# A 64-key by 96-query band for the product with V, a Newton step kept in PSUM, and a new table of places

## The reference

```python
def local_attention(q, k, v):          # window 32, 16 heads of 64
    # bk2, bv2: each window of 32 queries sees its own 32 keys and the 32 before
    mask = (it < jb) | (it > jb + w) | (jb == -1)
    sim = einsum('bhwie,bhwje->bhwij', bq, bk2) * 8.0
    sim = where(mask, -finfo.max, sim)
    attn = softmax(sim, -1)
    return einsum('bhwij,bhwje->bhwie', attn, bv2)

def ffn_layer(x, g, bln, W1, b1, W2, b2):
    mu = x.mean(-1); var = ((x - mu) ** 2).mean(-1)
    xn = (x - mu) / sqrt(var + 1e-05) * g + bln
    a, gate = split(xn @ W1 + b1, 2)
    return a * gelu(gate) @ W2 + b2

for i in range(6):
    x = attn_layer(shift_tokens(x), ...) + x
    x = ffn_layer(shift_tokens(x), ...) + x
```

## Time and profile before

| | |
|---|---|
| time, median of 3 | 3551.12 us (3550.79 to 3555.56) |
| span of the profiled execution | 3553.3 us |
| PE busy | 3325.9 us (94%), 65032 matmul records |
| DVE / ACT / POOL busy | 2737.3 (77%) / 2545.5 (72%) / 2041.5 us (57%) |
| granted clock of PE, mean | 0.984 of 2.4 GHz |
| stretch from 600 to 3500 us: PE, DVE, ACT, POOL | 2750.62, 2368.64, 2168.89, 1974.79 us of 2900 |

### The profile page before, as it was taken

One profiled execution on the slowest core, in us unless ns is written; L12 is line 12 of the kernel. 1 busy time (PEld: TensorE's weight loads), 2 busy tenths in 40 slices (PEclk: granted clock), 3 DMA queues, 4 the chain that ended last, 5 costly groups with the idle time before them and its releaser, 6 DMA issues.

```text
span 3553.3 us, 149054 instructions
## 1 busy us (share of the span) xinstructions
PE 3325.9 (94%) x65032; PEld 2107.6 (59%) x65032; DVE 2737.3 (77%) x3420; ACT 2545.5 (72%) x5866; POOL 2041.5 (57%) x1557
## 2 busy tenths in 40 slices
PE   7999987999999999999999999999999999999996
PEld 3444434666666666666666666666666666666663
DVE  3656557888887878888788878788888878788883
ACT  4667655777777777777777767677777777787774
POOL 0000006766676666766666666667676667676661
PEclk9999998999999999999999999999999999999998
DMA  3223224333333333433333333334333333333330
GB/s 109 76 71 84 75 61 141 135 127 127 134 133 133 118 127 130 140 131 129 119 122 136 130 124 127 127 124 143 126 130 126 121 136 125 135 127 131 129 122 24
DMA packets 247337, 423.34 MB, mean 119 GB/s; under 512 B 71966, under 2 KB 110108, under 8 KB 246556
## 3 DMA queue, kind: packets, MB, share of 16 engines
q1 hardware_dynamic: 220368, 397.28, 33.1%
q10 hardware_dynamic: 26316, 16.52, 1.6%
HBM read 124.21 MB, written 7.34 MB: 37 GB/s over the span
## 4 chain that ended last, share of the span: by engine, by line
PE 64%; DVE 17%; issue 7%; ACT 5%; POOL 5%; DMA 1%; SPq 1%; DVEq 0%; POOLq 0%; ACTq 0%
PE PS L535 64%; DVE TPB L932 5%; DVE MX L956 2%; ACT SC L1237 1%; DVE NV L947 1%; POOL K L1324 1%; POOL Q L1342 1%; DMA RB<-root_scratch 1%; POOL K L1342 1%; DVE PP L977 1%; DVE PX L978 1%; DVE NV L945 1%; DVE H L800 1%; DVE H L1000 1%; DVE NV L949 1%
## 5 line engine op out<-in xcount | busy, mean ns | idle before, releaser
L932 DVE SCALAR_TENSOR_TENSOR TPB<-PS,VEC,C 128x1024 f32<-128x1024 f32 x768 | 961.8, 1270 | 102.0 <-ACT SX L1213 95.0
L1237 ACT ACTIVATE SC<-PS,BQ,RQ 128x64 f32<-128x64 f32 x3072 | 979.5, 436 | 40.7 <-DVE BQ L961 40.3
L1213 ACT ACTIVATE SX<-PS 128x512 f32<-128x512 f32 x768 | 461.5, 620 | 391.4 <-PE PS L535 388.4
L1324 POOL TENSOR_TENSOR K<-K,RB 128x512 f32<-128x512 f32 x384 | 497.2, 1295 | 283.1 <-DMA RB<-root_scratch 278.4
L1347 POOL TENSOR_TENSOR SC<-SC,RC 128x1024 f32<-128x1024 f32 x192 | 366.3, 1908 | 480.2 <-DVE RC L969 478.8
L535 PEld LDWEIGHTS PS<-PP,VV 32*64 32x64 f32 x24576 | 433.7, 133 | 278.6 <-issue 276.3
L535 PE MATMUL PS<-PP,VV 32*64 32x64 f32 (+1 forms) x24576 | 541.2, 223 | 7.8 <-issue 6.2
L1342 POOL TENSOR_TENSOR K<-TPB,TR 128x512 f32<-128x512 f32 x384 | 496.4, 1293 | 0.0
L1342 POOL TENSOR_TENSOR Q<-TPB,TR 128x512 f32<-128x512 f32 x384 | 495.5, 1290 | 0.0
L535 PE MATMUL PS<-LXH,LH 128*128 128x512 f32 x768 | 371.3, 484 | 85.2 <-DVE TPB L932 68.4
L535 PE MATMUL PS<-K,Q 64*32 64x64 f32 (+1 forms) x24576 | 302.2, 224 | 49.5 <-issue 48.0
(11 more groups left out here) (167 smaller groups left out, 5809.8 us busy)
## 6 DMA issues: line engine op xcount, KB each, us to landing
TR<-TPB SPq DMA_DIRECT2D x768, 256.0 KB, 2.7
RB<-root_scratch SPq DMA_DIRECT2D x768, 128.0 KB
PP<-PX SPq DMA_DIRECT2D x192, 192.0 KB, 2.6
WS<-in_wqkv ACTq DMA_DIRECT2D x72, 128.0 KB, 2.4
PP<-PX SPq DMA_DIRECT2D x192, 48.0 KB, 2.5
QA<-TH SPq DMA_DIRECT2D x128, 64.0 KB, 2.1
QA<-TL SPq DMA_DIRECT2D x128, 64.0 KB, 2.1
KA<-TH SPq DMA_DIRECT2D x128, 64.0 KB, 2.1
```

Source lines behind the costliest of these rows:

```text
L932: e.scalar_tensor_tensor(TPB[:, n % 3:4 + n % 2:3 + n % 2 - n % 3, w, :], g, VEC[:, l, 9 + w:10 + w], C[:, at:at + 1024].rearrange("p (o c ...
L1213: e.activation(SX[i % 3][:, :], bk("PJ", key)[:, :], ACT.Square).then_inc(sem["pj_act"], 1)
L1237: p = e.activation(SC[m % 2][:, g, :, :].rearrange("p x k -> p (x k)"), bank[s][:, at:at + 64], ACT.Exp, bias=BQ[m % 2][:, g:g + 1], scale ...
L1324: e.tensor_tensor(dst, dst, RB[n % 2][:, :], ALU.mult).then_inc(sem["pr_pool"], 1)
```

## The change

Four things change.

1. **The band.** `PP` gets three places per head and window instead of two. Partitions 0 to 63 hold the 64 keys of windows j and j+1 (j even within its four), and the three places are the queries of windows j, j+1 and j+2: own keys and the keys before, with zeros in the two corners that a 64 by 96 block has and the band has not. POOL fills both PP with zeros once (before the first `NP`). Both transposes now write to tiles of their own, `PX[0]` and `PX[1]`, and SP carries both to PP: four DMAs of 32 partitions for the one and four for the other, instead of two DMAs.
2. **PV in two rounds** of 16 matmuls of 64 rows by 64 columns that move 96 columns (64 at the last window). The two row halves of a round write to different banks (`x = (t + rho) % 2`), and the second round swaps them. The matmuls of a step fall from 64 to 32, its records from 128 to 64.
3. **The feed-forward norm's Newton step in PSUM.** All three instructions of `rsqrt` write to the bank that F2 wrote; ACT's logarithm and exponential stay in H[0]; the tiles FX and EZ go. `F3` reads the root from the bank. So the bank is held until `F3` is through (`"f3_dve", u + 1`). The other layer norms use the same function: their first two results now stay in PSUM too, and their bank is held until the third instruction instead of the first.
4. **A new `PLACE` table**, with two places for PV instead of four.

```diff
-    "LS": 221.000, ... "PV": (4.410, 5.233, 5.448, 5.789), "PVn": 6.127,
+    "LS": 220.298, ... "PV": (4.733, 5.318), "PVn": 6.035,
...
-        o.put("N2", kind, b, banks=[(None, kind + "_root", 3, 1)])
-        o.keep(o.bank["N2", (kind, b), 0], kind + "_root", 3 * b + 1)
+        o.put("N2", kind, b, banks=[(None, kind + "_root", 3, 3)])
+        o.keep(o.bank["N2", (kind, b), 0], kind + "_root", 3 * b + 3)
...
-        lay(z + P["F2"], group, "F2", u, "f2_dve", 3 * u + 1)
+        lay(z + P["F2"], group, "F2", u, "f3_dve", u + 1)
...
-        PP = [sb(f"PP{i}", [128, 2, 16, 32]) for i in range(2)]
-        PX = sb("PX", [128, 16, 32])
+        PP = [sb(f"PP{i}", [128, 3, 16, 32]) for i in range(2)]
+        PX = [sb(f"PX{i}", [128, 16, 32]) for i in range(2)]
...
                 elif st == "PX":
                     m, = key
-                    a, z = PX, PP[m % 2]
+                    z = PP[m % 2]
+                    if m == 0:
+                        on.wait_ge("band_pool", 2)
                     if m > 1:
-                        on.wait_ge("pv_pe", 4 * m - 4)
+                        on.wait_ge("pv_pe", 2 * m - 2)
+                    on.wait_ge("tt_dve", 2 * m + 1)
+                    for r in range(4):
+                        k = slice(32 * r, 32 * r + 32)
+                        e.dma_start(z[k, r % 2, :, :], PX[0][k, :, :]).then_inc(sem[f"px_in{m % 2}"], 16)
                     on.wait_ge("tt_dve", 2 * m + 2)
-                    e.dma_start(z[0:96, 1, :, :], a[32:128, :, :]).then_inc(sem[f"px_in{m % 2}"], 16)
-                    e.dma_start(z[96:128, 1, :, :].rearrange("p (x c) a -> p x c a", c=4)[:, :, 0:3, :],
-                                a[0:32, :, :].rearrange("p (x c) a -> p x c a", c=4)[:, :, 1:4, :]).then_inc(sem[f"px_in{m % 2}"], 16)
+                    for r in range(1, 4):
+                        e.dma_start(z[32 * r - 32:32 * r, 1 + (r + 1) % 2, :, :],
+                                    PX[1][32 * r:32 * r + 32, :, :]).then_inc(sem[f"px_in{m % 2}"], 16)
+                    e.dma_start(z[96:128, 2, :, :].rearrange("p (x c) a -> p x c a", c=4)[:, :, 0:3, :],
+                                PX[1][0:32, :, :].rearrange("p (x c) a -> p x c a", c=4)[:, :, 1:4, :]).then_inc(sem[f"px_in{m % 2}"], 16)
...
                     for c in range(4):
-                        for x in range(2):
+                        for t in range(2):
                             for s in range(2):
-                                r = (rho + 2 * x + s) % 4
-                                j = 4 * c + r
-                                w = min(2, 16 - j)
+                                x = (t + rho) % 2
+                                j = 4 * c + 2 * t
+                                w = min(3, 16 - j)
                                 h = 2 * ((2 * p + x) % 8) + s
-                                y = mm(bank[2 + x][64 * s:64 * s + 64, 32 * j:32 * j + 32 * w],
-                                       VV[32 * r:32 * r + 32, c, 64 * h:64 * h + 64],
-                                       PP[p % 2][32 * r:32 * r + 32, 0:w, 8 * s + 4 * x + c, :],
-                                       rho == 0 and c == 0, rho == 3 and c == 3, skip_group_check=True)
+                                k = slice(64 * t, 64 * t + 64)
+                                y = mm(bank[2 + x][64 * s:64 * s + 64, 32 * j:32 * j + 32 * w], VV[k, c, 64 * h:64 * h + 64],
+                                       PP[p % 2][k, 0:w, 8 * s + 4 * x + c, :], rho == 0 and c == 0, rho == 1 and c == 3,
+                                       skip_group_check=True)
...
-            def rsqrt(v, u, x, step, done, r):
+            def rsqrt(v, x, y, step, done, r):
                 on.wait_ge(step, 2 * r + 2)
-                e.scalar_tensor_tensor(u, v, EPS, x, ALU.add, ALU.mult).then_inc(sem[done], 1)
+                e.scalar_tensor_tensor(v, v, EPS, x, ALU.add, ALU.mult).then_inc(sem[done], 1)
                 on.wait_ge(done, 3 * r + 1)
-                e.scalar_tensor_tensor(u, u, -0.5, x, ALU.mult, ALU.mult).then_inc(sem[done], 1)
+                e.scalar_tensor_tensor(v, v, -0.5, x, ALU.mult, ALU.mult).then_inc(sem[done], 1)
                 on.wait_ge(done, 3 * r + 2)
-                e.scalar_tensor_tensor(x, u, 1.5, x, ALU.add, ALU.mult).then_inc(sem[done], 1)
+                e.scalar_tensor_tensor(y, v, 1.5, x, ALU.add, ALU.mult).then_inc(sem[done], 1)
...
                     if m:
-                        on.wait_ge(f"px_in{(m - 1) % 2}", 32 * ((m - 1) // 2) + 32)
-                    if m > 1:
-                        on.wait_ge("pv_pe", 4 * m - 4)
+                        on.wait_ge(f"px_in{(m - 1) % 2}", 128 * ((m - 1) // 2) + 128)
                     on.wait_ge("np_pool", m + 1)
-                    e.transpose(PP[m % 2][:, 0, :, :], SC[m % 2][:, :, 1, :]).then_inc(sem["tt_dve"], 1)
-                    e.transpose(PX[:, :, :], SC[m % 2][:, :, 0, :]).then_inc(sem["tt_dve"], 1)
+                    e.transpose(PX[0][:, :, :], SC[m % 2][:, :, 1, :]).then_inc(sem["tt_dve"], 1)
+                    e.transpose(PX[1][:, :, :], SC[m % 2][:, :, 0, :]).then_inc(sem["tt_dve"], 1)
...
-                    rsqrt(bk("F2", key)[:, :], H[0][:, :], FX[:, :], "f2_act", "f2_dve", u)
+                    rsqrt(bk("F2", key)[:, :], H[0][:, :], bk("F2", key)[:, :], "f2_act", "f2_dve", u)
...
-                    e.tensor_tensor(H[2][:, :], H[1][:, :], FX[:, :], ALU.mult).then_inc(sem["f3_dve"], 1)
+                    e.tensor_tensor(H[2][:, :], H[1][:, :], bk("F2", key)[:, :], ALU.mult).then_inc(sem["f3_dve"], 1)
```

More of the change, by code:

```diff
@@ L29 @@
 PLACE = {
[13 rows of a table removed]
[8 rows of a table added]
+    "AQd": -0.283, "AV": (-11.276, -0.033), "AVa": -0.352, "AS": -1.210, "ASa": -1.501, "ASd": -1.358, "AY": 0.853,
+    "AE": 2.043, "AEa": 3.123, "AR": (14.319, 25.541), "AI": (24.544, 25.073, 27.040), "AM": (28.693, 0.806),
+    "AMd": -0.620, "AO": (30.433, 0.719), "NM": (36.253, 37.657, 37.185), "AZ": 39.606,
+    "NX": (43.040, 44.810, 45.102), "AW": 47.360,
 }
@@ L294, in order @@
                 lay(n + P["S3"][i], o.put, "S3", m, i)
+            for i in range(2):
                 lay(n + P["PV"][i], o.put, "PV", m, i)
@@ L379, in build @@
         ES = sb("ES", [128, L])
-        EZ = sb("EZ", [128, L])
         SC = [sb(f"SC{i}", [128, 16, 2, 32]) for i in range(2)]
-        PP = [sb(f"PP{i}", [128, 2, 16, 32]) for i in range(2)]
-        PX = sb("PX", [128, 16, 32])
+        PP = [sb(f"PP{i}", [128, 3, 16, 32]) for i in range(2)]
+        PX = [sb(f"PX{i}", [128, 16, 32]) for i in range(2)]
         XCH = sb("XCH", [128, L], F32R)
@@ L386, in build @@
         H = [sb(f"H{i}", [128, L]) for i in range(3)]
-        FX = sb("FX", [128, L])
         AOf = AO[0][:, :, :].rearrange("p a b -> p (a b)")
@@ L427, in nroot @@
         def nroot(kind):
-            return EZ if kind == "end" else NZ[("in", "mid", "x").index(kind)]
+            return ES if kind == "end" else NZ[("in", "mid", "x").index(kind)]
         def nused(kind, b):
@@ L730, in tensor_program @@
                         on.wait_ge("vp_act", 8 * u + 4 * half + 4)
-                        on.wait_ge(f"px_in{p % 2}", 32 * (p // 2) + 32)
-                        on.wait_ge("tt_dve", 2 * p + 1)
+                        on.wait_ge(f"px_in{p % 2}", 128 * (p // 2) + 128)
                         if p:
@@ L735, in tensor_program @@
                     else:
-                        on.wait_ge("pv_pe", 4 * p + rho)
+                        on.wait_ge("pv_pe", 2 * p + 1)
                     for c in range(4):
-                        for x in range(2):
+                        for t in range(2):
                             for s in range(2):
-                                r = (rho + 2 * x + s) % 4
-                                j = 4 * c + r
-                                w = min(2, 16 - j)
+                                x = (t + rho) % 2
+                                j = 4 * c + 2 * t
+                                w = min(3, 16 - j)
                                 h = 2 * ((2 * p + x) % 8) + s
-                                y = mm(bank[2 + x][64 * s:64 * s + 64, 32 * j:32 * j + 32 * w],
-                                       VV[32 * r:32 * r + 32, c, 64 * h:64 * h + 64],
-                                       PP[p % 2][32 * r:32 * r + 32, 0:w, 8 * s + 4 * x + c, :],
-                                       rho == 0 and c == 0, rho == 3 and c == 3, skip_group_check=True)
+                                k = slice(64 * t, 64 * t + 64)
+                                y = mm(bank[2 + x][64 * s:64 * s + 64, 32 * j:32 * j + 32 * w], VV[k, c, 64 * h:64 * h + 64],
+                                       PP[p % 2][k, 0:w, 8 * s + 4 * x + c, :], rho == 0 and c == 0, rho == 1 and c == 3,
+                                       skip_group_check=True)
                     y.then_inc(sem["pv_pe"], 1)
@@ L832, in vector_program @@
                     kind, b = key
```

(11 more changed lines are left out.)

## The result

The changed kernel takes **3882.83 us** (median of 5 runs, 3863.9 to 3886.3); the kernel before took 3552.73 us beside it. The ratio is 1.092 (95% interval 1.090 to 1.094): 330 us slower, where 3458 us was forecast, and outside the range. The profiled execution spans 3862.1 us.

The account below looks back on a forecast made before the run. PE sets the pace (busy 94%, DVE 77%), with an occasional late DVE result. Terms -154 + 88 - 12 - 14 - 20 + 15 + 4 = -93 us take the 3553.3 us span to 3460, median 3458 us; range 3385 to 3535.

Parts of the forecast that it names:

- Less cover elsewhere: Term: PE has 0.8 us less work a step before reusing banks, adding 15 us (0 to 60) of TPB waits.
- PV in two rounds: Term: on PE, two rounds of 0.84 us replace four of 0.62 us a step, 154 us less.
- F2's bank: Term: PE's PJ waits for F3 instead of L798, 1.9 us longer in each unit, 88 us more.
- the bank wait is absorbed: Rival, 20%: less than half of the 88 us of PE's wait for F2's bank stays; time 3408 us.
- Newton step in PSUM: Term: on DVE, two Newton instructions lose 0.2 to 0.3 us each in the mean, 14 us less.
- "Issue": Term: PE's 63.6 us of stops that nothing in the profile explains shrink with fewer records, 20 us less.
- give back: Term: behind the wait for F2's bank, PE waits less for DVE's rotary products, 12 us less (0 to 25).
- DVE takes over: Rival, 15%: DVE turns PE's gain into TPB waits, 60 us instead of 15, no issue gain; time 3523 us.
- Layer norms: Term: the other norms' bank is held two Newton instructions longer, 4 us more (0 to 10).
- DMA queue: Term: eight DMAs of PP instead of two fit SP's queue before the next TR; cost 0, bound 60 us.
- SP is late: Rival, 10%: RB and TR queue behind eight DMAs, POOL scales K late, scores wait; 3650 us at 1 us a step.

Follow-up runs that it names:

- e1: The changed kernel with one number moved, the second table preload TB from 16.015 to 16.140, behind the last gelu: 3481.2 us, ratio 0.982.
- e11: e9 with F3 back at 15.347, the feed-forward norm's Newton step in SBUF and F2's bank freed early: 3491.8 us, ratio 0.984.
- e4: The kernel before with the feed-forward Newton step in PSUM, its bank held till F3, F3 ahead of the rotary products: 3653.4 us, ratio 1.031.
- e9: e1 with the place table of the kernel before, PV at 4.410 and 5.448, F3 at 14.640: 3510.7 us, ratio 0.990.
- e3: e1 with the feed-forward norm's Newton step in SBUF and F2's bank freed by its first instruction: 3499.3 us, ratio 0.988.
- e6: e1 with the feed-forward norm's Newton instructions and F3 ahead of the two transposes on DVE: 3491.2 us, ratio 0.985.
- e5: e1 with SP's eight DMAs of PP placed behind the root write and the next TR: 3939.8 us, ratio 1.111.
- e7: e6 with the two transposes behind the two rotary products and the eight DMAs of PP at 2.900: 3902.5 us, ratio 1.100.
- e10: e1 with SP's eight DMAs of PP behind the root write but still ahead of TR: 3728.3 us, ratio 1.051.
- e12: e11 with SP's eight DMAs of PP behind the root write and ahead of TR: 3712.0 us, ratio 1.046.

## Why the prediction was wrong

**The failed step** is the last sentence of "Less cover elsewhere": the table of places "moves SS ahead of PV and leaves DVE's row as it was, so I give it nothing of its own". It put at nothing what cost some 400 us. I had compared the order on PE and on DVE and never on ACT, which was 25% free. On ACT one number of that table moved a table load between two gelus. Priced from the kernel before it would have been 8 loads x 1283 ns x 48 = 493 us of ACT's time; ACT had 731 us free in 2900, so no busy share forbade it to be free. But DVE and PE wait for ACT's results, and 402 us came through (e1). The Trainium skill (ScalarE: Activation LUTs, Table sets: the hidden batching unit) has the advice that would have led there, to group activations by table set; it also has Ln followed by Exp at one load, as one set holds both. That does not hold for the changed kernel, whose rows have a load ahead of each (1497.01, 1498.64).

**By terms, on e1, the changed kernel without the mishap.** Each is for 600 to 3400 us against the kernel before, or for 48 units:
- *PV in two rounds*, -154: right as PE's work. Sixteen rounds of 0.62 us less eight of 0.81 are 3.44 us a unit, 165 us; the 32 columns more cost 23 ns a pass, not 28. The row halves do run beside each other. As time it was wrong: alone the band gives 55 us (e11), since PE then waits for DVE.
- *F2's bank*, +88: right in size. L997's 99.8 us stand where L798 had 14.1: 86 more. As a price it was wrong both ways. In the old order, without the band, it costs 110 us (e4, with the gain of the Newton step in PSUM already in it); where the band has made PE early it costs 19 us (e11 to e9), and neither freeing the bank (e3) nor an earlier F3 (e6) gains anything. So the rival "the bank wait is absorbed" is right in its price; its time of 3408 did not come, as PV's gain shrank with it.
- *Newton step in PSUM*, -14: right in size. The second and third instruction took 938 and 823 ns in the kernel before and take 699 each, 17 us in 48 units; against e3 it is 25 us with F3. It is DVE's time, and no run shows how much of it reaches PE.
- *"Issue"*, -20: 61.5 to 10.0, 51 us off, more than twice the term. It stays in e4 (65.4), where PV is as before, and falls in e9 and e11 (22.5, 18.8), where PV has two rounds in the old places: it goes with PV's small matmuls.
- *Less cover* and *give back*, +15 and -12: TPB went from 58.1 to 20.0, 38 us off. PE now waits at F3 instead; in e11, where it does not, TPB's wait is 149 us. That is the rival "DVE takes over", and e11 shows it, at 55 us of gain where the rival kept 28.
- *Layer norms*, +4: right in size. Over its whole run e1's PE waits 6.3 us, seven times, for the third Newton instruction on NZ (L807), in the kernel before never. With the old places (e9) it is 5.5 us there and 7.6 at the last norm, "end", on which the prediction had nothing.
- *DMA queue*, 0: wrong. In e1 PE waits 44.3 us for K, before 0.6. SP's queue in e1:

```profile
1519.14 2.48 SPq L527 DMA_DIRECT2D PP<-PX  x4
1521.66 1.87 SPq L530 DMA_DIRECT2D PP<-PX  x3
1523.56 0.63 SPq L532 DMA_DIRECT2D PP<-PX  x1
1524.31 2.79 SPq L506 DMA_DIRECT2D root_scratch<-NV  x4
1527.19 1.16 SPq L498 DMA_DIRECT2D TR<-TPB  x2
1528.45 1.21 SPq L516 DMA_DIRECT2D RB<-root_scratch  x2
```

Eight DMAs hold SP 5.05 us, 0.63 each, and behind them queue the store of NV's norms, TR and RB without a gap. POOL, in the same kernel, stands for RB, and the scores for POOL:

```profile
1534.30 1.29 POOL L1327 TENSOR_TENSOR K<-K,RB 128x512 f32<-128x512 f32 x1 [5.18 <-DMA RB<-root_scratch]
```

POOL's wait for RB grew from 257.9 to 391.3 us, of which 44 reach PE. It "fits by half a microsecond" was read off one step; e1's trace has steps where it doesn't, the one above among them. It is inside my bound of 60. The rival "SP is late" was named, and e5, e7, e10 and e12 made it large.
- *The clock*, no term: 0.97 for 0.99 in this stretch. Two hundredths of PE's 2614 us are 52 us, an estimate. The whole run bears it out: PE is busy 3213.3 us for 3325.9, 113 less where PV's rounds alone are 165 shorter.

The sum: -165 + 86 + 44 - 38 - 51 = -124, and +52 for the clock is -72; the profiled executions of e1 and of the kernel before, from which the terms are read, lie 72 us apart, the medians 62. So without the table loads the time of 3481 would have been within the range, 23 us above the forecast, and the change -62 for -93.

That this is so near is in part luck. The parts taken one after another do not behave as the sum has them: the band alone gives -55 (e11), the bank held and the Newton step in PSUM then add some 20 (e9), and the new places take 30 off (e1). The forecast had -154 for the first, +74 for the second and nothing for the third.

What stays open is what sets e1's clock. PE does wait longer in sum there than in the kernel before (182 us for 135 in this stretch), but in e11 it waits longer still (211 us) at a clock of 0.978 over the run, against e1's 0.966. The waits differ in length: in e11 those for TPB are 0.9 us in the mean, e1 has one of 2.2 us for F3 in each unit. Behind some of these, not all, the clock is seen low: 0.64 from 1030.95 to 1033.43 us, behind a wait of 2.04, and 1.00 from 2038.90 to 2041.00, behind one of 1.97.

## What to carry to other kernels

A table of numbers is code for every engine: before a price of nothing is given, compare the order on all of them, and count the instructions that no line asks for, table loads first. Here one load that changed places with an activation brought eight more a unit. A wait that is taken away is worth its length only if nothing else on the same producer is late; ask what it meets next. A DMA's place in a queue is set by what stands ahead of it: putting eight behind one store that waits, in every second step, cost this kernel 220 and 247 us.

## What the runs showed of the hardware

- A table load takes 1283 ns in every group; it starts 0.01 us behind the activation ahead of it and is followed at once by its own (1497.01, 1498.31).
- Matmuls on 64 by 64 tiles with 96 columns: a round of 32 records in 0.81 us, eight passes of 101 ns. A pass of 64 columns took 78 ns.
- DVE with both tensors in SBUF, 128x512: 928, 872 and 808 ns in e3, 938, 823 and 715 ns in the kernel before; with one in PSUM 699, 699 and 687 ns, the same in the changed kernel, e1 and e4.
- SP issues the eight DMAs of PP in 5.05 us, 0.63 us each.
- PE's clock was at 0.53 in the 1.4 us behind a wait of 3.35 us, and at 1.00 from 3.6 us behind the wait's end on. In e4, with one wait of 2.5 us in each unit, PE is idle 57 us more than before and busy 38 us more with the same records.
